# Turning the rounded tokens of a feed-forward stage by transposing transfers, with two banks for the down product and the loads ahead on ScalarE's queue

## The chip, the core and the metric

The kernel runs on one core of a Trainium2 chip. A core has TensorE (PE, matrix products, results in PSUM banks), VectorE (DVE), ScalarE (ACT), GpSimd (POOL) and SyncE (SP), which each run their own list of instructions in order and meet through semaphores. Transfers are issued from an engine's queue and carried out by 16 DMA engines that all queues share. The metric is the time of one execution in microseconds of the device, the median of several runs.

## The reference

Two transformer layers on x of 8 x 256 tokens x 512. Each layer is x + attention(layernorm(x)), then x + feed-forward(layernorm(x)); layer 0 has multi-head causal cross-attention and a quantised feed-forward network, layer 1 has latent attention and a mixture of 8 experts. The change lies in layer 0's feed-forward network:

```python
def _act_quant(x):
    scale = 127.0 / jnp.clip(jnp.max(jnp.abs(x), axis=-1, keepdims=True), 1e-05)
    return jnp.clip(jnp.round(x * scale), -128.0, 127.0) / scale      # its value
def _weight_quant(w):
    scale = 1.0 / jnp.clip(jnp.mean(jnp.abs(w)), 1e-05)
    return jnp.clip(jnp.round(w * scale), -1.0, 1.0) / scale          # its value
def _bitlinear(x, w):
    return jnp.einsum('bsd,fd->bsf', _act_quant(x), _weight_quant(w))
h = jax.nn.silu(_bitlinear(x, W1))      # 512 -> 2048
return _bitlinear(h, W2)                # 2048 -> 512
```

## The kernel before

The program is a row of blocks with a barrier between them. `layer0_attention` is followed by `layer0_feed_forward`, which first rounds both weight matrices (`quantise_weights`) and then works through the tokens. After it come `layer1_attention`, whose first block (`score_weights`, L1065) waits for four large weights loaded ahead (`ahead_in`), and `layer1_experts`.

The feed-forward block has 16 tiles of 128 tokens. Its order is written out by hand: each engine runs `step(t, par)` for t from -3 to 15 (L915), and `has(t, n)` says whether tile t + n exists. For a tile:

- GpSimd normalises it into `y` (L1001). VectorE takes the largest absolute value of each token, works out the scale and rounds the tile to `xq`, 128 x 512 in bf16 (`quantise_tokens`, L1025 to L1034), three steps ahead.
- TensorE turns the four 128 x 128 pieces of `xq` into the PSUM tile `xT` (L969), at the end of a step, and ScalarE copies them to `xqT` (L994). The copy is the stationary operand of the up product.
- TensorE makes the up product, 16 matmuls into four PSUM banks (L954), two steps ahead. Each half waits until ScalarE has taken the half before out of the bank (`silued`). ScalarE applies Silu with the scale (L990).
- VectorE reduces the hidden units to a maximum (L1021, 128 x 2048) and makes their scale; ScalarE scales them and adds a constant that rounds (`hr`, L984); VectorE takes the constant off (`hq`, L1039). TensorE turns `hq` in 16 pieces into `hT` (L944), ScalarE copies these in two halves to `hqT` (L979).
- TensorE makes the down product, 16 matmuls into the bank `down` (L963). VectorE scales it and adds it to the tokens (L1016), then takes the new statistics (L105, L107).

So TensorE's step is: turn hidden t, up t + 2, down t, turn tokens t + 3. VectorE's step is: add the output t - 1, maximum and scale of the hidden t + 1, round tokens t + 3, round hidden t + 1, statistics t - 1. SP issues only the four loads ahead (L932 to L935), at the block's head.

Of the kernel before, what the change touches and what calls it, by code (L numbers as in the profile page):

```python
# [13 lines left out]
BF16 = mybir.dt.bfloat16  # L14
U32 = mybir.dt.uint32
ALU = mybir.AluOpType
ACT = mybir.ActivationFunctionType
AX = mybir.AxisListType

P = 128  # L20
B, S, D = 8, 256, 512
TPB = S // P
TILES = B * TPB
DC = D // P
CTX = 128
DMA = 16
# [5 lines left out]
FC = F // P  # L32
# [849 lines left out]
def layer0_feed_forward(nc, io, X, mv, rstd, identb, store, w1_raw, w1_in, ahead, ahead_in):  # L882
    with Memory(nc, "b") as m:
        w2_raw = store.place("w2_raw", 8, [P, FC, D])
        w1, w2 = store.place("w1", 18, [P, DC, F], BF16), store.place("w2", 22, [P, FC, D], BF16)
# [6 lines left out]

        y, yr = [m.sb(f"y{i}", [P, D]) for i in range(2)], m.sb("yr", [P, D])
        xq = [m.sb(f"xq{i}", [P, D], BF16) for i in range(2)]
        xqT = m.sb("xqT", [P, DC, P], BF16)
        s1, s2 = m.sb("s1", [P, 2]), m.sb("s2", [P, 2])
        h = [m.sb(f"h{i}", [P, F]) for i in range(2)]
        hr, hq = m.sb("hr", [P, F]), m.sb("hq", [P, F], BF16)
        hqT = m.sb("hqT", [P, FC, P], BF16)
        amax, unit, q_scale = m.sb("amax", [P, 2]), m.sb("unit", [P, 2]), m.sb("q_scale", [P, 2])  # L900
        stats = m.sb("stats", [P, 6])
        up = m.ps("up", [P, F])
        xT = m.ps("xT", [P, DC, P], BF16)
        hT = m.ps("hT", [P, FC, P], BF16)
        down = m.ps("down", [P, D])
        y_ready, x_quant, x_turned, x_copied = m.sem("y_ready"), m.sem("x_quant"), m.sem("x_turned"), m.sem("x_copied")
        upped, silued = m.sem("upped"), m.sem("silued")
        h_scaled, h_rounded, h_quant = m.sem("h_scaled"), m.sem("h_rounded"), m.sem("h_quant")
        h_turned, h_copied, downed, added = m.sem("h_turned"), m.sem("h_copied"), m.sem("downed"), m.sem("added")
        HALF = FC // 2  # L910

        def all_steps(eng, step):


            for t in range(-3, TILES):  # L915
                step(t, t % 2)

        def has(t, ahead):

            return 0 <= t + ahead < TILES  # L920

        def after(eng, sem, n):

            if n > 0:
                eng.wait_ge(sem, n)

        with m.block() as block:
            @block.sync
            def _(sp):

                wq, kcq, wqr, kckv = ahead
                sp.dma_start(kcq, io["kcq"].rearrange("h (c p) k -> p h c k", p=P)).then_inc(ahead_in, DMA)  # L932
                sp.dma_start(wqr, io["wqr"].rearrange("h (c p) r -> p h c r", p=P)).then_inc(ahead_in, DMA)
                sp.dma_start(wq, io["wq1"].rearrange("(h k) d -> k h d", k=P)).then_inc(ahead_in, DMA)
                sp.dma_start(kckv, io["kckv"].rearrange("h k d -> k h d")).then_inc(ahead_in, DMA)  # L935

            @block.tensor
            def _(pe):
                def step(t, par):
                    if has(t, 0):  # L940
                        pe.wait_ge(h_quant, t + 1)
                        after(pe, h_copied, 2 * t)
                        for c in range(FC):
                            last = pe.transpose(hT[:, c, :], hq[:, c * P:(c + 1) * P], identb[:, :])  # L944
                            if c == HALF - 1:
                                last.then_inc(h_turned, 1)
                        last.then_inc(h_turned, 1)
                    if has(t, 2):
                        pe.wait_ge(x_copied, t + 3)
                        for n in range(4):  # L950
                            if n % 2 == 0:
                                after(pe, silued, 2 * t + 3 + n // 2)
                            for c in range(DC):
                                last = pe.matmul(up[:, n * D:(n + 1) * D], xqT[:, c, :], w1[:, c, n * D:(n + 1) * D],  # L954
                                                 start=c == 0, stop=c == DC - 1)
                            if n % 2:
                                last.then_inc(upped, 1)
                    if has(t, 0):
                        after(pe, added, t)
                        for c in range(FC):  # L960
                            if c % HALF == 0:
                                pe.wait_ge(h_copied, 2 * t + 1 + c // HALF)
                            last = pe.matmul(down[:, :], hqT[:, c, :], w2[:, c, :], start=c == 0, stop=c == FC - 1)  # L963
                        last.then_inc(downed, 1)
                    if has(t, 3):
                        pe.wait_ge(x_quant, t + 4)
                        after(pe, x_copied, t + 3)
                        for c in range(DC):
                            last = pe.transpose(xT[:, c, :], xq[1 - par][:, c * P:(c + 1) * P], identb[:, :])  # L969
                        last.then_inc(x_turned, 1)  # L970
                all_steps(pe, step)

            @block.scalar
            def _(act):
                def step(t, par):
                    if has(t, 0):
                        for i in range(2):
                            act.wait_ge(h_turned, 2 * t + i + 1)
                            act.activation(hqT[:, i * HALF:(i + 1) * HALF, :], hT[:, i * HALF:(i + 1) * HALF, :], ACT.Copy  # L979
                                           ).then_inc(h_copied, 1)  # L980
                    if has(t, 1):
                        act.wait_ge(h_scaled, t + 2)
                        after(act, h_quant, t + 1)
                        act.activation(hr[:, :], h[1 - par][:, :], ACT.Copy, scale=q_scale[:, 1:2], bias=MAGIC  # L984
                                       ).then_inc(h_rounded, 1)
                    if has(t, 2):
                        for n in range(2):
                            act.wait_ge(upped, 2 * t + n + 5)
                            cols = slice(n * F // 2, (n + 1) * F // 2)
                            act.activation(h[par][:, cols], up[:, cols], ACT.Silu, scale=s1[:, par:par + 1]  # L990
                                           ).then_inc(silued, 1)
                    if has(t, 3):
                        act.wait_ge(x_turned, t + 4)
                        act.activation(xqT[:], xT[:], ACT.Copy).then_inc(x_copied, 1)  # L994
                all_steps(act, step)

            @block.gpsimd
# [7 lines left out]
            def _(dve):  # L1005
                def scales(i):

                    dve.drain()
                    dve.tensor_scalar(unit[:, i:i + 1], amax[:, i:i + 1], 1e-5, 1.0 / 127.0, ALU.max, ALU.mult)
                    dve.drain()  # L1010
                    return dve.reciprocal(q_scale[:, i:i + 1], unit[:, i:i + 1])

                def add_output(t, par):
                    dve.wait_ge(downed, t + 1)
                    xt = X[:, t, :]
                    dve.scalar_tensor_tensor(xt, down[:, :], s2[:, par:par + 1], xt, ALU.mult, ALU.add  # L1016
                                             ).then_inc(added, 1)

                def scale_hidden(t, par):
# [3 lines left out]
                    dve.tensor_scalar(s2[:, par:par + 1], unit[:, 1:2], mean[:, 1:2], None, ALU.mult)  # L1023

                def quantise_tokens(t, par):  # L1025
                    after(dve, x_turned, t - 1)
                    dve.wait_ge(y_ready, t + 1)
                    dve.tensor_reduce(amax[:, 0:1], y[par][:, :], AX.X, ALU.max, apply_absolute_value=True)
                    scales(0)
                    dve.tensor_scalar(s1[:, par:par + 1], unit[:, 0:1], mean[:, 0:1], None, ALU.mult)  # L1030
                    dve.drain()
                    dve.tensor_scalar(yr[:, :], y[par][:, :], q_scale[:, 0:1], MAGIC, ALU.mult, ALU.add)
                    dve.drain()
                    dve.tensor_scalar(xq[par][:, :], yr[:, :], -MAGIC, 127.0, ALU.add, ALU.min).then_inc(x_quant, 1)  # L1034
# [9 lines left out]
                def step(t, par):  # L1044
                    if has(t, -1):
                        add_output(t - 1, 1 - par)
                    if has(t, 1):
                        scale_hidden(t + 1, 1 - par)
                    if has(t, 3):
                        quantise_tokens(t + 3, 1 - par)  # L1050
                    if has(t, 1):
                        quantise_hidden(t + 1)
                    else:
                        dve.drain()
                    if has(t, -1):
                        new_stats(t - 1)
                all_steps(dve, step)
                add_output(TILES - 1, (TILES - 1) % 2)
                dve.drain()
                new_stats(TILES - 1)  # L1060
# [836 lines left out]
```

## Time and profile before

| | us |
|---|---|
| median of 3 runs | 1128.49 (1125.04 to 1131.27) |
| the profiled execution | 1127.68 |
| its span, first to last instruction | 1125.9 |
| TensorE busy in the span | 994.8 (88%) |
| VectorE, ScalarE busy | 763.1 (68%), 651.4 (58%) |
| GpSimd busy | 283.4 (25%) |
| feed-forward block, from its first load's issue to its last output add | 325.64 to 471.51 |

A row of the timeline gives the start, the length, the engine, the line, the operation, what it writes and reads, and how many instructions are merged; in brackets stands how long the engine was idle before it and what released it. A matmul's end is modelled, so the start of the next group on TensorE is the better mark. A row of the stretches gives the busy time of each engine with its count, the granted clock of TensorE as a share of the full one, the share of the DMA engines, and GB/s.

### The profile page before, as it was taken

To read this page: it belongs to the slowest core of one execution; us is meant where nothing else is said; L and a number is where in the kernel's file an instruction comes from. 1 tells how busy PE (TensorE), PEld (TensorE's weight loads), DVE (VectorE), ACT (ScalarE), POOL (GpSimd) and SP (SyncE) were. 2 spreads that over 40 slices of the span, in tenths; PEclk is the share of its full clock that TensorE was granted. 3 is DMA by queue.
4 is the path that set the end of the run, shared out by engine and by line. 5 is a ranking of instruction groups with operands and counts; after the bars stand their busy time and mean duration, and the time that the engine had idled before them with its cause. 6 is when DMAs were issued, how large, how long until landed. Compare 5 with 4: busy or idle time off the path is not lost. (4 is left out here: it accounts for less than half of the span.)

```text
span 1125.9 us, 20668 instructions
## 1 busy us (share of the span) xinstructions
PE 994.8 (88%) x7516; PEld 782.9 (70%) x7516; DVE 763.1 (68%) x1654; ACT 651.4 (58%) x1691; POOL 283.4 (25%) x276
## 2 busy tenths in 40 slices
PE   5799999997129999886999999899998999999586
PEld 5678888876014555534888888788887888888485
DVE  6757666664757998435676767577775767777466
ACT  4657777765547878454555555355554555555275
POOL 5765565343033332021001010010101001000372
PEclk9989999999659999987999999999999999999889
DMA  7210000000438000141000000000000000000013
GB/s 263 98 67 6 7 2 2 2 1 1 149 105 249 1 1 2 38 169 57 1 1 19 2 20 2 3 20 1 20 1 23 1 1 1 1 1 2 0 39 113
DMA packets 20091, 41.95 MB, mean 37 GB/s; under 512 B 1168, under 2 KB 4496, under 8 KB 19472
## 3 DMA queue, kind: packets, MB, share of 16 engines
q1 hardware_dynamic: 19984, 40.53, 10.8%
q8 instruction: 67, 1.10, 0.4%
q14 instruction: 40, 0.33, 0.1%
HBM read 36.33 MB, written 4.19 MB: 36 GB/s over the span
## 5 line engine op out<-in xcount | busy, mean ns | idle before, releaser
L1214 POOL TENSOR_TENSOR c_ctx_raw<-c_ctx_raw,c_table 128x1024 f32<-128x1024 f32 x8 | 19.0, 2379 | 448.7 <-PE c_bank_b L1358 366.5
L1440 ACT ACTIVATE probs<-c_score,c_neg_max 128x256 f32<-128x256 f32 x256 | 119.2, 480 | 15.4 <-DVE c_neg_max L1501 15.4
L1426 ACT ACTIVATE c_h<-c_bank_b 128x512 fp32r<-128x512 f32 x64 | 38.3, 598 | 153.6 <-PE c_bank_b L1358 153.6
L559 POOL TENSOR_TENSOR a_probs<-a_probs,a_inv 128x256 f32<-128x256 f32 (+1 forms) x128 | 102.7, 830 | 90.5 <-DVE a_inv L660 90.4
L451 ACT ACTIVATE a_probs<-a_s,a_neg_max 128x128 f32<-128x128 f32 (+1 forms) x256 | 104.4, 435 | 32.3 <-DVE a_neg_max L648 31.9
L1491 DVE TENSOR_TENSOR c_l<-c_bank_b,c_h 128x512 fp32r<-128x512 f32 x64 | 44.3, 692 | 99.2 <-ACT c_h L1426 99.2
L1431 ACT ACTIVATE c_pT_h<-c_turn 128x512 fp32r<-128x512 f32 x128 | 69.9, 596 | 63.4 <-PE c_turn L1348 63.4
L44 PE MATMUL c_acc<-VO_h,c_l 128*128 128x512 f32 x256 | 100.9, 394 | 1.9 <-DVE c_l L1491 1.9
L46 PE MATMUL c_acc<-VO_h,c_h 128*128 128x512 f32 x256 | 100.5, 393 | 0.0
L45 PE MATMUL c_acc<-VO_l,c_h 128*128 128x512 f32 x256 | 100.0, 391 | 0.0
L1501 DVE TENSOR_REDUCE c_neg_max<-c_score 128x2 f32<-128x512 f32 x128 | 82.0, 682 | 9.7 <-PE c_score L1337 8.8
L1496 DVE TENSOR_TENSOR c_pT_l<-c_turn,c_pT_h 128x512 fp32r<-128x512 f32 x128 | 82.1, 681 | 2.3 <-ACT c_pT_h L1431 2.3
L44 PE MATMUL c_bank_a<-c_yT_h,A_l 128*128 128x256 f32 x256 | 78.3, 306 | 1.4 <-DVE c_yT_l L1482 1.4
L1509 DVE TENSOR_SCALAR probs<-probs,c_inv 128x256 f32<-128x256 f32 x256 | 75.7, 359 | 5.1
L45 PE MATMUL c_bank_a<-c_yT_l,A_h 128*128 128x256 f32 x256 | 73.1, 286 | 0.0
L46 PE MATMUL c_bank_a<-c_yT_h,A_h 128*128 128x256 f32 x256 | 72.9, 285 | 0.0
L1348 PE MATMUL c_turn<-g_ident,probs 128*128 128x128 f32 x512 | 72.1, 286 | 0.7 <-DVE probs L1509 0.7
L648 DVE TENSOR_REDUCE a_neg_max<-a_s 128x2 f32<-128x256 f32 (+1 forms) x128 | 63.5, 549 | 10.5 <-PE a_s L317 9.9
L1001 POOL TENSOR_SCALAR b_y<-g_x,g_mean_var,g_rstd 128x512 f32<-128x512 f32 x16 | 44.3, 2768 | 100.6 <-DVE b_xq L1034 65.4
L1487 DVE TENSOR_TENSOR c_qk_l<-c_bank_a,c_qk_h 128x512 fp32r<-128x512 f32 x64 | 44.0, 687 | 29.9 <-ACT c_qk_h L1422 29.7
L1348 PEld LDWEIGHTS c_turn<-g_ident,probs 128*128 128x128 f32 x512 | 57.2, 144 | 8.8 <-DVE probs L1509 1.4
L954 PE MATMUL b_up<-w,b_xqT 128*128 128x512 bf16 x256 | 60.9, 393 | 2.2 <-ACT b_xqT L994 2.2
(253 smaller groups left out, 2866.6 us busy)
## 6 DMA issues: line engine op xcount, KB each, us to landing
w_raw<-in_w SPq DMA_DIRECT2D x1, 4096.0 KB, 13.8
w_raw<-in_w SPq DMA_DIRECT2D x4, 1024.0 KB, 8.8
wq<-in_wq SPq DMA_DIRECT2D x1, 4096.0 KB, 22.8
c_ctx_raw<-in_ctx SPq DMA_DIRECT2D x8, 512.0 KB, 3.6
wo<-in_wo SPq DMA_DIRECT2D x1, 4096.0 KB, 14.3
out<-g_x SPq DMA_DIRECT2D x16, 256.0 KB, 2.1
g_x<-in_x SPq DMA_DIRECT2D x7, 512.0 KB, 6.6
wq_raw<-in_wq SPq DMA_DIRECT2D x4, 256.0 KB, 4.5
```

The source lines that it names most:

```text
L44: pe.matmul(out, ll, rh, start=start and n == 0, stop=False)
L45: pe.matmul(out, lh, rl, start=False, stop=False)
L46: last = pe.matmul(out, lh, rh, start=False, stop=stop and n == len(pairs) - 1)
L451: last = act.activation(probs[i % 2][:, 2 * pair + j, at], s[:, 2 * pair + j, at], ACT.Exp, bias=neg_max[:, pair, q, j:j + 1], accum_out=s ...
L559: last = pool.tensor_tensor(p, p, inv[:, pair, q, :].unsqueeze(2).broadcast_to([P, 2, (q + 1) * P]), ALU.mult)
L648: last = dve.tensor_reduce(neg_max[:, pair, q, :], s[:, 2 * pair:2 * pair + 2, q * P:(2 * q + 1) * P], AX.X, ALU.max, negate=True)
L1348: last = pe.transpose(turn[k][:, hq * P:(hq + 1) * P], probs[p % 2][:, hq, k * P:(k + 1) * P], ident[:, :])
L1431: act.activation(pT_h[:, k, :], turn[k][:, :], ACT.Copy).then_inc(turn_hi, 1)
L1440: last = act.activation(probs[p % 2][:, i, :], score[h][:, t, :], ACT.Exp, bias=neg_max[:, i:i + 1], accum_out=sums[:, i:i + 1])
L1496: dve.tensor_tensor(pT_l[:, k, :], turn[k][:, :], f32(pT_h[:, k, :]), ALU.subtract).then_inc(turn_lo, 1)
L1501: dve.tensor_reduce(neg_max[:, 2 * h:2 * h + 2], score[h][:, :, :], AX.X, ALU.max, negate=True).then_inc(maxed, 1)
L1509: last = dve.tensor_scalar(probs[p % 2][:, i, :], probs[p % 2][:, i, :], inv[:, i:i + 1], None, ALU.mult)
```

## The change

1. The four 128 x 128 pieces of a rounded token tile are turned by four transfers with `transpose=True` that SP issues, straight into `xqT`, which now has two buffers. TensorE's token transposes, the PSUM tile `xT`, ScalarE's copy and the semaphore `x_copied` go. `x_turned` becomes two semaphores, one for each buffer, that count 16 for each transfer. The up product waits for four transfers of its tile; SP waits for the rounding, and for the up product two tiles earlier before it writes its buffer again.
2. The down product alternates between two PSUM banks, and so waits for the output add of two tiles earlier.
3. The four loads ahead are issued from ScalarE's queue, ahead of its first step, and no longer from SP's.

The hidden units are turned by TensorE as before.

```diff
-        xqT = m.sb("xqT", [P, DC, P], BF16)
+        xqT = [m.sb(f"xqT{i}", [P, DC, P], BF16) for i in range(2)]
...
-        xT = m.ps("xT", [P, DC, P], BF16)
         hT = m.ps("hT", [P, FC, P], BF16)
-        down = m.ps("down", [P, D])
+        down = [m.ps(f"down{i}", [P, D]) for i in range(2)]
...
+        X_TURN = DC * DMA
...
             @block.sync
             def _(sp):
 
-                wq, kcq, wqr, kckv = ahead
-                sp.dma_start(kcq, io["kcq"].rearrange("h (c p) k -> p h c k", p=P)).then_inc(ahead_in, DMA)
...
+                for t in range(TILES):
+                    sp.wait_ge(x_quant, t + 1)
+                    after(sp, upped, 2 * (t - 1))
+                    for c in range(DC):
+                        sp.dma_start(xqT[t % 2][:, c, :], xq[t % 2][:, c * P:(c + 1) * P], transpose=True).then_inc(x_turned[t % 2], DMA)
...
                     if has(t, 2):
-                        pe.wait_ge(x_copied, t + 3)
+                        pe.wait_ge(x_turned[par], ((t + 2) // 2 + 1) * X_TURN)
...
-                        after(pe, added, t)
+                        after(pe, added, t - 1)
...
-                            last = pe.matmul(down[:, :], hqT[:, c, :], w2[:, c, :], start=c == 0, stop=c == FC - 1)
+                            last = pe.matmul(down[par][:, :], hqT[:, c, :], w2[:, c, :], start=c == 0, stop=c == FC - 1)
                         last.then_inc(downed, 1)
-                    if has(t, 3):
-                        pe.wait_ge(x_quant, t + 4)
-                        after(pe, x_copied, t + 3)
-                        for c in range(DC):
-                            last = pe.transpose(xT[:, c, :], xq[1 - par][:, c * P:(c + 1) * P], identb[:, :])
-                        last.then_inc(x_turned, 1)
...
-                    if has(t, 3):
-                        act.wait_ge(x_turned, t + 4)
-                        act.activation(xqT[:], xT[:], ACT.Copy).then_inc(x_copied, 1)
+
+                wq, kcq, wqr, kckv = ahead
+                act.dma_start(kcq, io["kcq"].rearrange("h (c p) k -> p h c k", p=P)).then_inc(ahead_in, DMA)
+                act.dma_start(wqr, io["wqr"].rearrange("h (c p) r -> p h c r", p=P)).then_inc(ahead_in, DMA)
+                act.dma_start(wq, io["wq1"].rearrange("(h k) d -> k h d", k=P)).then_inc(ahead_in, DMA)
+                act.dma_start(kckv, io["kckv"].rearrange("h k d -> k h d")).then_inc(ahead_in, DMA)
                 all_steps(act, step)
...
                 def quantise_tokens(t, par):
-                    after(dve, x_turned, t - 1)
+                    after(dve, x_turned[t % 2], t // 2 * X_TURN)
```

The order of ScalarE's instructions at the block's head, of the kernel before, with what each waits for:

```order
L973 UNCONDITIONAL_BRANCH [waits barrier_Pool_Activation_PE_DVE_SP_release]
L994 ACTIVATE b_xqT<-b_xT 128x512 [waits b_x_turned]
L990 ACT_TABLE_LOAD
L990 ACTIVATE b_h<-b_up,b_s 128x1024 [waits b_upped] x2
L994 ACTIVATE b_xqT<-b_xT 128x512 [waits b_x_turned]
L984 ACTIVATE b_hr<-b_h,b_q_scale 128x2048 [waits b_h_scaled]
```

and of the changed kernel, at the same place:

```order
L967 UNCONDITIONAL_BRANCH [waits barrier_Pool_Activation_PE_DVE_SP_release]
L988 DMA kcq<-in_kcq 128x48x128
L989 DMA wqr<-in_wqr 128x48x64
L990 DMA wq_50<-in_wq 128x16x512
L991 DMA kckv<-in_kckv 128x16x128
L984 ACT_TABLE_LOAD
L984 ACTIVATE b_h<-b_up,b_s 128x1024 [waits b_upped] x2
L978 ACTIVATE b_hr<-b_h,b_q_scale 128x2048 [waits b_h_scaled]
```

The four loads stand ahead of the loading of the Silu table and of the first Silu; the copies of the turned tokens are gone.

SP's list at the same place, the difference from before to after:

```order
 L928 UNCONDITIONAL_BRANCH [waits barrier_Pool_Activation_PE_DVE_SP_release]
-L932 DMA kcq<-in_kcq 128x48x128
-L933 DMA wqr<-in_wqr 128x48x64
-L934 DMA wq_50<-in_wq 128x16x512
-L935 DMA kckv<-in_kckv 128x16x128
+L935 DMA_TRANSPOSE b_xqT<-b_xq 128x128 [waits b_x_quant]
+L935 DMA_TRANSPOSE b_xqT<-b_xq 128x128 x3
+L935 DMA_TRANSPOSE b_xqT<-b_xq 128x128 [waits b_x_quant]
+L935 DMA_TRANSPOSE b_xqT<-b_xq 128x128 x3
+L935 DMA_TRANSPOSE b_xqT<-b_xq 128x128 [waits b_upped,b_x_quant]
+L935 DMA_TRANSPOSE b_xqT<-b_xq 128x128 x3
```

SP's queue now holds 64 transposing transfers, four for each of the 16 tiles, the first of each tile behind the waits.

TensorE's list from the head into the first full step, the difference from before to after:

```order
 L937 UNCONDITIONAL_BRANCH
-L969 MATMUL b_xT<-g_identb,b_xq 128x128 x4
-L954 MATMUL b_up<-w_4887,b_xqT 128x512 x16
-L969 MATMUL b_xT<-g_identb,b_xq 128x128 x4
-L954 MATMUL b_up<-w_4887,b_xqT 128x512 x16
-L969 MATMUL b_xT<-g_identb,b_xq 128x128 x4
+L954 MATMUL b_up<-w_4887,b_xqT 128x512 x32
 L944 MATMUL b_hT<-g_identb,b_hq 128x128 x16
 L954 MATMUL b_up<-w_4887,b_xqT 128x512 x16
 L963 MATMUL b_down<-w_4888,b_hqT 128x512 x16
-L969 MATMUL b_xT<-g_identb,b_xq 128x128 x4
 L944 MATMUL b_hT<-g_identb,b_hq 128x128 x16
```

Nothing else moves: a full step is the hidden turn, up and down, now without the four token transposes behind them.

## Rows read from the trace of the kernel before

**Rows 1.** The page: its span.
```profile
span 1125.9 us, 20668 instructions
```
**Rows 2.** Stretches: PE, PEld, DVE, ACT, POOL busy (count), clock, DMA share, GB/s.
```profile
362.00:459.00 97.00, 97.00 (x638) 51.67 (x637) 85.40 (x163) 77.28 (x73) 27.90 (x10) 1.00 0.00 1
459.00:466.00 7.00, 4.71 (x36) 2.42 (x34) 4.82 (x8) 3.97 (x4) 0.00 (x0) 1.00 0.00 0
```
**Rows 3.** Timeline of one period, TensorE, then VectorE.
```profile
387.23 3.62 PE L954 MATMUL b_up<-w,b_xqT 128*128 128x512 bf16 x16
...
394.13 0.39 PE L969 MATMUL b_xT<-g_identb,b_xq 128*128 128x128 bf16 x4
394.36 1.06 PE L944 MATMUL b_hT<-g_identb,b_hq 128*128 128x128 bf16 x16
395.25 3.62 PE L954 MATMUL b_up<-w,b_xqT 128*128 128x512 bf16 x16
...
394.34 0.75 DVE L1016 SCALAR_TENSOR_TENSOR g_x<-b_down,b_s,g_x 128x512 f32<-128x512 f32 x1 [0.27 <-PE b_down L963]
...
399.67 0.43 DVE L1034 TENSOR_SCALAR b_xq<-b_yr 128x512 bf16<-128x512 f32 x1
```
**Rows 4.** Waits between 360 and 460 us: total, times, longest.
```profile
ACT b_hr L984 <- DVE b_q_scale L1011: 9.5, 12, 0.8
ACT b_xqT L994 <- PE b_xT L969: 9.5, 12, 0.8
```
**Rows 5.** Timeline of SP's queue at the block's head.
```profile
325.64 0.84 SPq L932 DMA_DIRECT2D kcq<-in_kcq  x1
326.93 9.24 SPq L933 DMA_DIRECT2D wqr<-in_wqr  x1
...
344.84 4.21 SPq L935 DMA_DIRECT2D kckv<-in_kckv  x1
```
**Rows 6.** Timeline of ScalarE at the block's head.
```profile
331.25 0.60 ACT L994 ACTIVATE b_xqT<-b_xT 128x512 bf16<-128x512 bf16 x1 [5.92 <-PE b_xT L969]
331.87 1.28 ACT L990 ACT_TABLE_LOAD   x1
335.36 1.11 ACT L990 ACTIVATE b_h<-b_up,b_s 128x1024 f32<-128x1024 f32 x1 [2.21 <-PE b_up L954]
337.09 1.11 ACT L990 ACTIVATE b_h<-b_up,b_s 128x1024 f32<-128x1024 f32 x1 [0.61 <-PE b_up L954]
```
**Rows 7.** Timeline of VectorE and TensorE, from the head to the last period.
```profile
338.23 2.29 DVE L1021 TENSOR_REDUCE b_amax<-b_h 128x1 f32<-128x2048 f32 x1 [5.02 <-ACT b_h L990]
338.74 3.63 PE L954 MATMUL b_up<-w,b_xqT 128*128 128x512 bf16 x16 [1.47 <-ACT b_xqT L994]
...
342.91 0.43 DVE L1034 TENSOR_SCALAR b_xq<-b_yr 128x512 bf16<-128x512 f32 x1
...
345.58 5.14 PE L954 MATMUL b_up<-w,b_xqT 128*128 128x512 bf16 x16
...
350.56 3.62 PE L963 MATMUL b_down<-w,b_hqT 128*128 128x512 bf16 x16
...
454.87 3.62 PE L963 MATMUL b_down<-w,b_hqT 128*128 128x512 bf16 x16
```
**Rows 8.** Transfers: queue instructions by line, issues by source, to landing.
```profile
L1615 SPq DMA_DIRECT2D out<-g_x x16: 332/332/375, 1087.8 to 1123.4; - x16
...
DMA to landing us min/median/max: 2.0/2.1/2.9
...
L123 SPq DMA_DIRECT2D w_raw<-in_w x4: 379/500/1262, 287.0 to 288.5; - x4
...
g_ident<-in_ident SPq DMA_DIRECT2D x1, 64.0 KB, 3.0
...
kckv<-in_kckv SPq DMA_DIRECT2D x1, 0.5 KB, 17.6
g_iota<-in_iota SPq DMA_DIRECT2D x1, 4.0 KB, 3.2
```

More of the change, by code:

```diff
@@ L902, in layer0_feed_forward @@
         up = m.ps("up", [P, F])
-        xT = m.ps("xT", [P, DC, P], BF16)
         hT = m.ps("hT", [P, FC, P], BF16)
-        down = m.ps("down", [P, D])
-        y_ready, x_quant, x_turned, x_copied = m.sem("y_ready"), m.sem("x_quant"), m.sem("x_turned"), m.sem("x_copied")
+        down = [m.ps(f"down{i}", [P, D]) for i in range(2)]
+        y_ready, x_quant, x_turned = m.sem("y_ready"), m.sem("x_quant"), [m.sem(f"x_turned{i}") for i in range(2)]
         upped, silued = m.sem("upped"), m.sem("silued")
@@ L929, in _ @@
             def _(sp):
-                wq, kcq, wqr, kckv = ahead
-                sp.dma_start(kcq, io["kcq"].rearrange("h (c p) k -> p h c k", p=P)).then_inc(ahead_in, DMA)
-                sp.dma_start(wqr, io["wqr"].rearrange("h (c p) r -> p h c r", p=P)).then_inc(ahead_in, DMA)
-                sp.dma_start(wq, io["wq1"].rearrange("(h k) d -> k h d", k=P)).then_inc(ahead_in, DMA)
-                sp.dma_start(kckv, io["kckv"].rearrange("h k d -> k h d")).then_inc(ahead_in, DMA)
+                for t in range(TILES):
[3 more added lines that the diff above has]
+                        sp.dma_start(xqT[t % 2][:, c, :], xq[t % 2][:, c * P:(c + 1) * P], transpose=True).then_inc(x_turned[t % 2], DMA)
             @block.tensor
@@ L953, in step @@
                             for c in range(DC):
-                                last = pe.matmul(up[:, n * D:(n + 1) * D], xqT[:, c, :], w1[:, c, n * D:(n + 1) * D],
+                                last = pe.matmul(up[:, n * D:(n + 1) * D], xqT[par][:, c, :], w1[:, c, n * D:(n + 1) * D],
                                                  start=c == 0, stop=c == DC - 1)
@@ L1015, in add_output @@
                     xt = X[:, t, :]
-                    dve.scalar_tensor_tensor(xt, down[:, :], s2[:, par:par + 1], xt, ALU.mult, ALU.add
+                    dve.scalar_tensor_tensor(xt, down[par][:, :], s2[:, par:par + 1], xt, ALU.mult, ALU.add
                                              ).then_inc(added, 1)
```

## The prediction

> **What bounds the kernel now.** I read the page first, then the busy time by stretches, one period of the feed-forward block in the timeline, its waits, and last the queues at the block's head. The profiled execution took 1127.68 us, of which 1125.9 are the span [rows 1]; the median of the three runs is 1128.49, so a sum made on the profile stands 0.8 us under it. The change touches one of four blocks, from the start of its loads at 325.64 [rows 5] on. From 362 to 459 TensorE is busy 97.00 of 97.00 us at the full granted clock, VectorE 85.40, ScalarE 77.28 [rows 2]. A tile takes 395.25 - 387.23 = 8.02 us there, from up product to up product; between lie down, the turning of the tokens (4 matmuls, 394.13) and that of the hidden units (394.36) [rows 3]. So the 4 token transposes own 0.23 us of a period. VectorE is close behind: it waits 0.27 us for down in this period, which leaves it 7.75 of its own. ScalarE waits for TensorE and for VectorE, 0.8 us each per tile [rows 4]. At the head it is different: ScalarE's first two Silus end at 338.20 and VectorE, idle until then, starts its maximum at 338.23 [rows 6, 7]. The head is a chain of dependences and not a full engine.
>
> **Turning off TensorE and ScalarE.** 16 x 4 transposes and 16 copies (0.60 us each) go. Only the TensorE part lies on the path: from the down at 350.56 to that at 454.87 there are 13 periods (104.31 / 13 = 8.02) [rows 7], times 0.23 = 3.0 us, if nothing takes its place. The copies stood in a ScalarE that waits 0.8 us twice in a period [rows 4]: nothing. The second bank for down is worth nothing, since VectorE's add (0.75 us from 394.34) is done long before the next down, which follows the up of 395.25.
>
> **The wait that comes instead.** up now waits for four transfers that SP issues once VectorE has rounded the tile. (SP's own second wait, for the up two tiles back, is over by then: that up ended in the period before.) Call L the time from the end of the rounding to the landing of the fourth. The rounding of rows 3 ends at 399.67 + 0.43 = 400.10; the up that used it started one period after 395.25, at 403.27. L must be under 3.17 us to keep 8.02, and under 2.7 for a period of 7.79. If it is longer, a ring closes: up starts at 387.23, down after it, VectorE's add at 394.34, then maximum and scale of the hidden units, then the rounding that ends at 400.10 and serves the up two tiles on. That is 12.87 us plus L for two tiles. A period is (12.87 + L) / 2, and each us of L over 3.17 costs half a us per tile. Behind this wait on TensorE stand up, down and the next hidden turn; VectorE's add waits for that down.
> No transposing transfer is in the trace. The nearest rows are plain transfers of SP's queue: issue 0.33 us at the shortest (output), 1.26 at the longest and 0.50 in the middle (w_raw); landing 2.0 at the shortest (output), 3.0 for 64 KB and 3.2 for 4 KB inward [rows 8]. Four in a row have three issues ahead of the last: L from 3 x 0.33 + 2.0 = 3.0 to 3 x 1.26 + 3.2 = 7.0. I take 3 x 0.50 + 3.0 = 4.5, the middle issue and the inward transfer nearest in size to a piece of 32 KB. Then (12.87 + 4.5) / 2 = 8.69, which is 0.67 over 8.02, times 13 = **+8.7 us** (ends: -1.1 at L = 3.0; +24.9 at 7.0, a period of 9.94). VectorE's 7.75 shortens nothing: it waits for down, which waits for up. The clock should hold: at 459 to 466, with TensorE busy 4.71 of 7.00 us, it was still granted 1.00, the upper of its two levels, 2.4 GHz [rows 2].
> The Trainium skill ("DMA: Bandwidth & Descriptors", Anatomy of one DMA) gives every transfer a fixed part of about 2.0 us, mostly the receipt of the last byte; this trace agrees with its 2.0 to 3.2 us [rows 8]. By 2.0 alone an estimate of L would be 3.5 and of the period 8.19.
>
> **The loads move in front of ScalarE's work.** SP issued the four loads from 325.64 to 344.84 + 4.21 = 349.05, and the second issue alone held the queue 9.24 us [rows 5]. SP had nothing else to do, so that was free. Now the same four stand in ScalarE's stream ahead of its table load and its first Silu. ScalarE works in order, so its table load starts at 349.05, not 331.87, and the Silus end at 349.05 + 1.28 + 2 x 1.11 = 352.55, not 338.20 [rows 6]. VectorE's maximum moves from 338.23 to about 352.55: **+14.3 us**. TensorE meanwhile has tile 0's up done and idles, so tile 1's up may run at the lower clock level, 5.14 us as the up at 345.58 [rows 7] did; started behind the first Silu at 351.4 it ends at 356.6, and the old end, 338.74 + 3.63, moved by 14.3 is 356.7: nothing is added. Nor does tile 0's turning show: it has until about 345. Bounds of this term: 14.3 if the queue holds ScalarE as it held SP; 0 if each issue is as short as the first (0.84), since four of those lie within the 5.92 us that ScalarE sat idle here [rows 6]. I take 14.3, since bytes, descriptors and the 16 DMA engines are the same.
> The Trainium skill says against this ("DMA: Bandwidth & Descriptors", Issuing engines are not separate DMA queues) that issuing from several engines saves only the sequencer's time, "which is usually small relative to the DMA itself". The row says otherwise: 23.4 us of issuing, with the last byte at 362.4. By the page the move would cost ScalarE little; that is case (b).
>
> **Turning while the loads run.** The DMA engines are in use until kckv lands at 344.84 + 17.6 = 362.4 [rows 5, 8]. Tile 2's rounding, ended at 343.34, and its up, at 345.58 [rows 7], both move by 14.3, to 357.6 and 359.9: 2.2 us for an L among loads. Its lower end is 3.0 (+0.8); its upper end, as long as that load's own landing, 17.6, is +15. I take 4.8, a little over the free case, since the pieces are small: **+2.6 us**. Later tiles are turned after 362.
>
> Sum: 1127.68 + 14.3 + 2.6 + 8.7 = 1153.3 as an execution like the profiled one, and 0.8 more against the median: **1154 us**.
>
> **Rivals.**
> (a) Transposing transfers are slow or follow each other one by one. At 2 us apart and 3.0 to land, L = 9.0, the period is 10.94, and +37.9 takes the place of 8.7: 1182. For it: a queue instruction can last 9.24 us when the engines are full, and nothing in the trace shows a transpose. Against: 32 KB each on idle engines (share 0.00 from 362 to 459 [rows 2]). It begins at L = 6, 1163 us.
> (b) ScalarE isn't held by its queue: 1127.68 + 2.6 + 8.7 = 1139.0. For it: only the first issue, 0.84 us, met free engines, and ScalarE's queue is otherwise empty. Against: the second issue waited with nothing ahead of it but the first.
> (c) The change does all that it removes and nothing comes instead, the case that isn't slower: ScalarE not held and L at most 2.7. TensorE's period falls to 7.79, just above VectorE's 7.75: 1127.68 - 3.0 = 1124.7. It needs four transfers issued and landed in 2.7 us where single ones took 2.0 to 3.2.
>
> **How the numbers follow.** Forecast (held, L of 3.0 to 6.0, own range 1141 to 1163): 0.57. (a): 0.25. (b): 0.13. (c): 0.05. The range from 1137 to 1176 takes in most of (b) and the nearer half of (a), and leaves out about 2 in 10. A measurement of this kernel tells 0.5%, 5.6 us, from no change: faster is under 1122.8, slower over 1134.1. (c) and the shortest of (b) are within: 0.07. Under 1122.8 lies no case: 0.02. Slower: 0.91.
>
> **What will show it.** Four issue rows on ScalarE's queue that end near 349 and the first Silu at about 350.3. TensorE idle ahead of up, released by a transfer of xqT, some 0.9 us a tile; the down products 8.7 us apart; ScalarE's wait for TensorE's token turn gone; TensorE's share of the stretch under 1. A turned piece landing in about 3 us. I am wrong if the first Silu starts before 340, if the issue rows on ScalarE are short, if the period is under 8.0 or over 9.5, or if the granted clock in the block's middle falls below 1.00.

## The result, and the profile after

The changed kernel takes 1173.48 us (median of 4 runs, 1170.78 to 1179.13) beside 1126.76 us of the kernel before (4 runs): a ratio of 1.0422, with a 95% interval of 1.036 to 1.0484. It is slower. The time lies in the forecast range, but the step is +46.7 us where 25.5 were forecast.

The page of the profiled execution after (1171.65 us) begins so; PEclk in its second part is the granted clock in 40 slices, in tenths. The second fence is the same row of the kernel before.

```profile
span 1169.9 us, 20586 instructions
...
PEclk9999999997568889898799999999999999999798
```

```profile
PEclk9989999999659999987999999999999999999889
```

Slices 14 to 16 lie in the block's middle in both: 9 9 9 before, 8 8 9 after. Over 105 us there the granted clock is 0.91 after (columns as in [rows 2], where it is 1.00):

```profile
385.00:490.00 105.00, 88.07 (x483) 42.59 (x482) 72.53 (x142) 60.59 (x50) 25.98 (x9) 0.91 0.06 13
```

The span grew by 44.0 us from that of [rows 1]. I cut both spans at the first GpSimd normalisation of the block (325.64 before, 321.19 after) and at the end of its last output add (471.51, 516.80). What lies ahead of the block is the same program in both and differs by 4.5 us in the other direction (over the eleven kernels of this document the block starts between 321.2 and 325.6); what lies behind is 654.4 and 653.1 us. The block itself went from 145.9 to 195.6: **+49.7 us**, the whole loss. Its head, up to the first down product, went from 24.9 to 45.7 (+20.8); the 13 periods from the first down to the fourteenth from 104.3 to 133.3 (+29.0); its tail is 16.6 in both. The two down products that bound the periods after (before: [rows 7]):

```profile
366.86 3.62 PE L963 MATMUL b_down<-w,b_hqT 128*128 128x512 bf16 x16
...
500.15 3.62 PE L963 MATMUL b_down<-w,b_hqT 128*128 128x512 bf16 x16
```

The head, in ScalarE's timeline of the kernel after; it answers to [rows 5, 6]:

```profile
321.19 0.87 ACTq L988 DMA_DIRECT2D kcq<-in_kcq  x1
...
322.52 9.62 ACTq L989 DMA_DIRECT2D wqr<-in_wqr  x1
332.17 10.48 ACTq L990 DMA_DIRECT2D wq<-in_wq  x1
...
342.86 4.37 ACTq L991 DMA_DIRECT2D kckv<-in_kckv  x1
347.26 1.28 ACT L984 ACT_TABLE_LOAD   x1 [4.43 <-issue]
348.56 2.12 ACT L984 ACTIVATE b_h<-b_up,b_s 128x1024 f32<-128x1024 f32 x2
```

ScalarE does nothing for 26.0 us but hand over loads. Its first two Silus end 29.5 us into the block, where they ended 12.6 us into it before.

Two tiles of the steady part, TensorE and VectorE's rounding in the timeline after; they answer to [rows 3]:

```profile
434.73 3.62 PE L954 MATMUL b_up<-w,b_xqT 128*128 128x512 bf16 x16
...
438.18 3.62 PE L963 MATMUL b_down<-w,b_hqT 128*128 128x512 bf16 x16
...
439.37 0.43 DVE L1031 TENSOR_SCALAR b_xq<-b_yr 128x512 bf16<-128x512 f32 x1
...
441.64 1.06 PE L944 MATMUL b_hT<-g_identb,b_hq 128*128 128x128 bf16 x16
...
445.89 5.31 PE L954 MATMUL b_up<-w,b_xqT 128*128 128x512 bf16 x16 [3.19 <-DMA b_xqT<-b_xq]
...
451.04 3.62 PE L963 MATMUL b_down<-w,b_hqT 128*128 128x512 bf16 x16
...
455.39 3.62 PE L954 MATMUL b_up<-w,b_xqT 128*128 128x512 bf16 x16
```

The rounding ends at 439.80 and the up that needs it starts at 445.89: L is 6.09 us, read up to the start of that up. The wait comes at every other tile. A tile with it takes 12.86 us from down to down (438.18 to 451.04), one without it 7.80 (451.04 to 458.84), the period that had been worked out for a TensorE without its token transposes. And the up behind the wait lasts 5.31 us, not 3.62. The stretches show the granted clock (columns as in [rows 2]):

```profile
441.80:445.80 4.00, 0.89 (x16) 0.72 (x13) 3.81 (x6) 2.46 (x3) 1.08 (x1) 1.00 0.11 25
445.80:447.50 1.70, 1.61 (x7) 0.66 (x7) 1.40 (x6) 1.49 (x1) 0.00 (x0) 0.82 0.00 0
447.50:451.00 3.50, 3.50 (x11) 1.35 (x10) 2.02 (x4) 1.11 (x1) 2.98 (x1) 0.60 0.09 19
451.00:454.00 3.00, 3.00 (x15) 1.37 (x14) 0.00 (x0) 1.11 (x1) 0.00 (x0) 1.00 0.13 27
```

After TensorE's idle 3.2 us the granted clock falls, in the up that follows, to a mean of 0.60 over 3.5 us, most of it at the lower of its two levels (1.2 GHz), and is back at 1.00 (2.4 GHz) with the down behind it. The 16 matmuls pay 1.7 us.

The transposing transfers themselves, from the view of the tile xqT of the kernel after; [rows 8] held only plain ones:

```profile
L935 SPq DMA_TRANSPOSE b_xqT<-b_xq x64: 1093/1232/1936, 326.1 to 492.6; - x64
...
DMA to landing us min/median/max: 2.2/2.3/9.5
```

So 3 x 1.23 + 2.3 = 6.0 us, the L of the timeline.

### The profile page after: what moved, and what is told of

Its sections match the earlier page's. It is cut to its first block and busy times, and to the rows that moved or that the text cites. A ratio compares the mean times of both kernels' runs of the same rounds, so it can differ in the third digit from the quotient of the medians.

```text
span 1169.9 us, 20586 instructions
## 1 busy us (share of the span) xinstructions
PE 1001.1 (86%) x7452; PEld 777.5 (66%) x7452; DVE 766.3 (66%) x1654; ACT 645.4 (55%) x1678; POOL 283.1 (24%) x276
## 5 line engine op out<-in xcount | busy, mean ns | idle before, releaser
L954 PE MATMUL b_up<-w,b_xqT 128*128 128x512 bf16 x256 | 74.5, 457 | 59.9 <-DMA b_xqT<-b_xq 52.7
L954 PEld LDWEIGHTS b_up<-w,b_xqT 128*128 128x128 bf16 x256 | 28.1, 114 | 100.6 <-DMA b_xqT<-b_xq 54.0
L1506 DVE TENSOR_SCALAR probs<-probs,c_inv 128x256 f32<-128x256 f32 x256 | 79.1, 373 | 5.1
```

What stands on the lines that cost most here:

```text
L954: last = pe.matmul(up[:, n * D:(n + 1) * D], xqT[par][:, c, :], w1[:, c, n * D:(n + 1) * D], start=c == 0, stop=c == DC - 1)
L1506: last = dve.tensor_scalar(probs[p % 2][:, i, :], probs[p % 2][:, i, :], inv[:, i:i + 1], None, ALU.mult)
```

## The experiments

Two theories stand against each other. The first has four causes that add: ScalarE held at the head, the latency L in a ring through VectorE, the clock that falls in the waits, and a turning that is slow beside the loads. The main rival is that the loads, moved and mixed with the turning, make all of it. In the table, head, 13 periods and block are in us as defined above, from the profiled execution; the ratio is to the kernel before, measured beside each.

| kernel | median us | ratio (95%) | head | 13 periods | block |
|---|---|---|---|---|---|
| before (four medians) | 1126.76 to 1128.34 | 1 | 24.9 | 104.3 | 145.9 |
| after | 1173.48 | 1.0422 (1.036 to 1.0484) | 45.7 | 133.3 | 195.6 |
| e1_loads_on_scalar | 1144.85 | 1.0157 (1.011 to 1.0204) | 41.8 | 104.3 | 164.4 |
| e2_loads_spread | 1166.74 | 1.0348 (1.0309 to 1.0388) | 38.8 | 133.8 | 189.2 |
| e3_one_transfer | 1149.01 | 1.02 (1.0155 to 1.0244) | 33.7 | 115.6 | 167.6 |
| e4_fill_the_wait | 1167.47 | 1.0368 (1.0307 to 1.0429) | 39.9 | 131.3 | 187.8 |
| e5_one_bank | 1171.06 | 1.0422 (1.0389 to 1.0455) | 38.9 | 133.7 | 189.2 |
| e6_loads_last | 1202.47 | 1.0668 (1.065 to 1.0685) | 33.7 | 133.1 | 183.5 |
| e7_one_transfer_loads_last | 1156.95 | 1.0266 (1.0247 to 1.0285) | 26.8 | 101.4 | 144.8 |
| e8_round_earlier | 1136.16 | 1.0086 (1.0062 to 1.0111) | 35.1 | 102.9 | 154.6 |
| e9_one_earlier_late_loads | 1124.67 | 0.9984 (0.9963 to 1.0006) | 26.5 | 102.4 | 147.2 |

**e1_loads_on_scalar.** The kernel before, with the loads' queue changed alone.

```diff
-                sp.dma_start(kcq, ...)      # and wqr, wq, kckv
+                act.dma_start(kcq, ...)     # and wqr, wq, kckv, ahead of all_steps(act, step)
```

> The kernel before with one part of the change: the four loads ahead are issued from ScalarE's queue instead of SP's; tokens are still turned by TensorE. Theory (the queue holds ScalarE as it held SP, 23.4 us from first to last issue): the first Silus end about 14 us later in the block, everything after is shifted, 1127 + 14 = 1141 us. Rival (in the changed kernel ScalarE was held because transposing transfers ran beside the loads): the issues are short here, first Silus at most 3 us later, 1127 to 1130 us.

+16.5 us (1144.85 to 1128.34). ScalarE's timeline in it:

```profile
324.16 0.88 ACTq L993 DMA_DIRECT2D kcq<-in_kcq  x1
...
325.49 9.43 ACTq L994 DMA_DIRECT2D wqr<-in_wqr  x1
334.95 8.17 ACTq L995 DMA_DIRECT2D wq<-in_wq  x1
...
343.34 4.03 ACTq L996 DMA_DIRECT2D kckv<-in_kckv  x1
347.42 0.60 ACT L990 ACTIVATE b_xqT<-b_xT 128x512 bf16<-128x512 bf16 x1 [4.11 <-issue]
```

The queue holds ScalarE for 23.2 us, as it held SP for 23.4 [rows 5], with no transposing transfer anywhere; the rival is out. It costs more than the 14 expected, since here the copy of the first turned tile stands behind the loads too, and the first up starts only behind it, at 348.47. The periods are untouched, 104.3.

**e2_loads_spread.** The changed kernel, with each load issued by ScalarE in a step of its own.

```diff
+                far = {-3: (kcq, ...), 1: (wqr, ...), 3: (wq, ...), 6: (kckv, ...)}
                 def step(t, par):
+                    if t in far:
+                        act.dma_start(*far[t]).then_inc(ahead_in, DMA)
```

> The changed kernel with its four loads issued by ScalarE one at a time, in steps -3, 1, 3 and 6, so that each meets an idle queue. Theory (two causes that add: ScalarE held at the head, and a ring closed by L = 6.1 us with a slow up product behind each long wait): issues under 1 us each, the head as in the kernel before within 4 us, 20.7 us for two tiles as in the changed kernel, so 13 x (10.3 - 8.0) = +30 and about 1157 to 1160 us. Rival (the loads are the cause of the whole loss, later tiles suffer from a late start): within 5 us of the kernel before.

The issues are short now:

```profile
322.91 0.89 ACTq L977 DMA_DIRECT2D kcq<-in_kcq  x1
361.97 0.73 ACTq L977 DMA_DIRECT2D wqr<-in_wqr  x1
382.37 0.42 ACTq L977 DMA_DIRECT2D wq<-in_wq  x1
415.86 0.72 ACTq L977 DMA_DIRECT2D kckv<-in_kckv  x1
```

The periods stay at 133.8, so the hold explains nothing of them. But the head fell only by 6.9, to 38.8, and the time is 7 us over the upper end that I had expected. The first tile was rounded at 327.82 and its up began at 339.46, 11.6 us later: four transfers beside kcq's load, which landed at 338.6. My head, "as before within 4 us", was a miss.

**e3_one_transfer.** As e2, with one transfer for a tile.

```diff
-                    for c in range(DC):
-                        sp.dma_start(xqT[t % 2][:, c, :], xq[t % 2][:, c * P:(c + 1) * P], transpose=True)...
+                    sp.dma_start(xqT[t % 2][:, :, :], xq[t % 2][:, :], transpose=True)...
```

> As e2_loads_spread, but one transposing transfer of 128 x 512 turns a tile in place of four of 128 x 128. Theory A (the 1.23 us in the queue are paid once for each instruction): L = about 1.2 + 2.3 = 3.5 us, the ring gives (12.9 + 3.5) / 2 = 8.2 us a tile, no long wait of TensorE and so no slow up, 1128 to 1133 us. Theory B (the queue's time goes by the blocks turned, 0.15 us for each 16 x 128 block): one issue holds 4.9 us, L stays near 6, 1157 us as e2_loads_spread.

```profile
L934 SPq DMA_TRANSPOSE b_xqT<-b_xq x16: 1189/1191/1308, 329.8 to 468.2; - x16
...
DMA to landing us min/median/max: 2.3/2.3/10.1
```

One instruction that turns 128 KB holds the queue 1.19 us and lands 2.3 us after its issue, the same as one that turns 32 KB. Theory A holds for the price, B is out, and L is 2.3 to 2.4 with no load beside it, shorter still than the 3.5 that I had added up: the 2.3 us to the landing include the 1.2 in the queue. Outside the loads the tiles follow at 7.80 us. The time is 16 us over what A expected. The block is 21.7 us longer than before's: 8.8 in the head, where tile 0 landed 10.2 us after its rounding, beside kcq's load; 11.3 in the periods; 1.7 in a last down at the lower clock. The waits in TensorE's timeline say where those of the periods are:

```profile
385.42 3.60 PE L953 MATMUL b_up<-w,b_xqT 128*128 128x512 bf16 x8 [6.48 <-DMA b_xqT<-b_xq]
...
414.64 5.31 PE L953 MATMUL b_up<-w,b_xqT 128*128 128x512 bf16 x15 [2.88 <-DMA b_xqT<-b_xq]
```

They stand right behind the issues of wq (374.64) and kckv (407.51). A transposing transfer beside a load lands late, up to 10.1 us, and the ring has no slack for that.

**e4_fill_the_wait.** As e2, with one bank for down, and matmuls in TensorE's wait; their result is not used.

```diff
+                        for _ in range(14 if t >= 0 and t % 2 == 0 else 0):
+                            pe.matmul(fill[:, :], w1[:, 0, 0:P], w1[:, 0, 0:D], start=True, stop=True)
                         pe.wait_ge(x_turned[par], ((t + 2) // 2 + 1) * X_TURN)
```

> As e2_loads_spread, with one bank for the down product and, in the bank that this frees, 14 matmuls of 128 x 512 on TensorE ahead of the wait for the turned tokens of tiles 2, 4, ... 14 (their result is not used), about 3.0 us, within the 3.2 us that TensorE waits there. Theory (the up product behind the wait runs slow because TensorE's clock falls in the wait): up takes 3.6 us in place of 5.0 to 6.4, 19.0 us for two tiles in place of 20.7, 10 us less than e2_loads_spread. Rival (up is slow for another reason, such as its operand just landed): same time as e2_loads_spread, up still over 5 us.

```profile
439.95 3.19 PE L950 MATMUL b_fill<-w 128*128 128x512 bf16 x13
443.31 3.63 PE L956 MATMUL b_up<-w,b_xqT 128*128 128x512 bf16 x16 [0.18 <-DMA b_xqT<-b_xq]
...
458.92 3.19 PE L950 MATMUL b_fill<-w 128*128 128x512 bf16 x13
462.81 3.63 PE L956 MATMUL b_up<-w,b_xqT 128*128 128x512 bf16 x16 [0.70 <-DMA b_xqT<-b_xq]
```

The up behind a filled wait takes 3.63 us with its operand just landed, so the slow up is the clock's doing and not its operand's. The granted clock around such an up, the one at 424.34, is 1.00:

```profile
423.90:428.00 4.10, 3.76 (x18) 1.68 (x18) 3.60 (x9) 2.79 (x2) 2.01 (x1) 1.00 0.04 8
```

The ring closes as worked out: from the up at 424.34 to the rounding that ends at 437.22 are 12.88 us, plus an L of 6.09, and two tiles take 18.97 (to 443.31); the next pairs take 19.50 and 19.61, with L at 6.61 and 6.73, against 20.65 without the filling. In the whole time it does not show, 1167.47 beside 1166.74: the 13 periods are only 2.5 us shorter, and my expectation of 10 us less was a miss. The fillings don't fit everywhere; a wait of 6.58 us beside wq's load fell on an odd tile, which had none, and at the head they delay an up. So the mechanism is shown; its price over the block, 10 us, is read from the rows of the kernel after and not from a time.

**e5_one_bank.** As e2, with a single bank.

```diff
-        down = [m.ps(f"down{i}", [P, D]) for i in range(2)]
+        down = m.ps("down", [P, D])
-                        after(pe, added, t - 1)
+                        after(pe, added, t)
```

> As e2_loads_spread, with a single bank for the down product, which waits for the output add of the tile before. Theory (the second bank is worth nothing, the add is done 3 us or more ahead of the next down product): the same time as e2_loads_spread, 1163 to 1170 us, no wait of TensorE or of its weight loads ahead of down. Rival (the ring makes the add late, so the second bank hides part of it): 1 us or more a tile longer, over 1175.

1171.06 us, ratio 1.0422 (1.0389 to 1.0455) beside e2's 1.0348 (1.0309 to 1.0388). The medians lie 4 us apart, and e5's is 1 us over my upper end. In the profiled executions the blocks are equal, 189.2 us each, and the periods 133.7 and 133.8. In both, weight loads ahead of down wait 1.8 us in all for the add, twice. I read it as no effect of the bank in the block, from one execution of each. The rows can't say where the 4 us lie: e5's profiled execution, 1164.34 us, is the shortest of its six and shorter than e2's, 1165.91. What makes them stays open.

**e6_loads_last.** The changed kernel, with the four loads issued by ScalarE behind its last step. The next block waits for them, so only the block is to be compared.

```diff
-                act.dma_start(kcq, ...)     # and wqr, wq, kckv
                 all_steps(act, step)
+                act.dma_start(kcq, ...)     # and wqr, wq, kckv
```

> The changed kernel with its four loads issued by ScalarE behind its last step of the block, so that nothing runs beside the turning; the next block then waits for them (known price about 20 to 30 us there). Read the block alone. Theory (ring with L = 6.1 us and the clock fall): every even tile's up behind a 3.2 us wait, 20.7 us for two tiles from the head to the end, first down about 27 to 30 us after the block's start in place of 45.7 (before: 24.9). Rival (the waits come from the loads beside it): no wait over 1 us, 7.8 us a tile.

```profile
437.52 5.31 PE L954 MATMUL b_up<-w,b_xqT 128*128 128x512 bf16 x16 [3.20 <-DMA b_xqT<-b_xq]
...
458.18 5.31 PE L954 MATMUL b_up<-w,b_xqT 128*128 128x512 bf16 x16 [3.20 <-DMA b_xqT<-b_xq]
```

458.18 - 437.52 = 20.66 with nothing beside the turning, and 133.1 us for the 13 periods: they owe nothing to the loads. The head is 33.7 us, more than the 27 to 30 I expected: it alone, with neither hold nor loads, is 8.8 over before's, from 6.2 us between rounding and up at tile 0 (before: 1.4) and 6.1 at tile 2 (before: 2.2). The ups behind both are slow, but so were before's, 5.15 and 5.14 us, so the clock adds nothing there. The late loads cost 36 us behind the block in the profiled execution, not 20 to 30.

**e7_one_transfer_loads_last.** e6 with one transfer for a tile.

> As e6_loads_last, with one transposing transfer a tile. Theory (one instruction costs 1.2 us of queue and lands 2.3 us after its issue, whether it turns 32 KB or 128 KB, and is slow only beside the loads): L = 2.4 us, no wait of TensorE, 7.80 us a tile throughout, the block 3 to 4 us shorter than before's 145.9, then the late loads' price of 20 to 30 us behind it. Rival (the one transfer was also slowed by itself in e3_one_transfer): the waits of 2.9 and 6.5 us seen there come again.

```profile
351.76 3.62 PE L962 MATMUL b_down<-w,b_hqT 128*128 128x512 bf16 x16
...
453.16 3.62 PE L962 MATMUL b_down<-w,b_hqT 128*128 128x512 bf16 x16
```

No wait for a transfer over 0.3 us after the first tile; the 13 periods are 101.4 us, which is 13 x 7.80, and the block 144.8, 1.1 shorter than before's, where I had expected 3 to 4. The transposes' 0.23 us a tile are there, 2.9 us in the periods; the head, 1.9 longer than before's, takes most of them back. The time, 1156.95 us, is longer than before's by what follows: behind the block the profiled execution takes 691.7 us (before: 654.4), as the next block waits for the late loads. The waits of e3 did not come again, so they were the loads'.

**e8_round_earlier.** As e2, four transfers a tile, with VectorE four steps ahead and three buffers.

```diff
-            for t in range(-3, TILES):
+            for t in range(-4, TILES):
-                        quantise_tokens(t + 3, 1 - par)
+                        quantise_tokens(t + 4, par)
-        xqT = [m.sb(f"xqT{i}", [P, DC, P], BF16) for i in range(2)]
+        xqT = [m.sb(f"xqT{i}", [P, DC, P], BF16) for i in range(3)]
```

> As e2_loads_spread (four transfers a tile, loads one at a time in steps -3, 1, 3 and 6), but VectorE rounds the tokens four steps ahead and not three, with three buffers of turned tokens. Theory (the loss is latency in a ring, not the capacity of the queue: 4 x 1.23 = 4.9 us of 7.8): the wait goes, 7.8 us a tile outside the loads, and only what the loads add (an L of 9 to 12) may show; 1126 to 1140 us. Rival (the queue or the DMA engines can't keep up): still over 9 us a tile, 1160.

```profile
356.33 3.62 PE L963 MATMUL b_down<-w,b_hqT 128*128 128x512 bf16 x16
...
459.22 3.62 PE L963 MATMUL b_down<-w,b_hqT 128*128 128x512 bf16 x16
```

The queue carries what it did in e2, 64 transfers of 1.23 us each, and the periods fall from 133.8 to 102.9 us. One wait is left behind the head, 1.29 us beside a load. The loss in the periods was latency in a ring and not the capacity of a queue. The head is still 35.1, 10.1 over before's: tile 0 is turned beside kcq's load, and its up starts 15.9 us into the block where before's started 6.3 us into it.

**e9_one_earlier_late_loads.** e8 with one transfer for a tile and the loads in steps 0, 3, 6 and 10.

> As e8_round_earlier with one transposing transfer a tile and the loads moved to steps 0, 3, 6 and 10, so that the first tiles are turned with nothing beside them. Theory: no wait of TensorE for a transfer at all, 7.80 us a tile, the block 3 us shorter than before's, 1124 to 1126 us, level with the kernel before or just ahead. Rival (an L beside a load is longer than the 10.5 us that the deeper pipeline covers): waits at the steps of the loads, 1130 or more.

```profile
378.84 3.63 PE L953 MATMUL b_up<-w,b_xqT 128*128 128x512 bf16 x16 [0.62 <-DMA b_xqT<-b_xq]
```

The best form of the idea: 1124.67 us, 0.9984 of the kernel before (0.9963 to 1.0006), no difference that can be told. A single wait of 0.62 us is left, where I had expected none. Its block is 1.3 us longer than before's: the periods give 1.9, the head costs 1.6, and its last down ran at the lower clock (5.29 us), for 1.7.

## Why the prediction was right, and where it was not

The direction and the range held, the range with 2.5 us to spare. The likeliest case held in kind, a ScalarE held by its queue and a ring that closes, but the step was 1.8 times the forecast. 1173.48 us lies outside that case's own range, 1141 to 1163, and the L of 6.09 just inside case (a), which was to begin at 6. Two of the signs of being wrong that the prediction named came: the period, 133.3 / 13 = 10.25 us, is over 9.5, and the granted clock in the block's middle is under 1.00. That the number fell within the range is so in part luck: the range had been stretched for slower transfers, and a part of what filled it, 10.7 us, is a slower clock that no case had. And the block alone grew by 49.7; in the profiled executions 5.8 us of that are offset outside the block. By its steps, against the block's +49.7 us:

- **The term for the loads in front of ScalarE (+14.3)** was right in mechanism, and 2.6 short. The Silus end 16.9 us later in the block; the issues took 26.0 us with the turning beside them, where they took 23.2 in e1 without it. Case (b) is out: e1 shows these 23.2 us of issuing in ScalarE's own stream. The Trainium skill's "usually small relative to the DMA itself" ("DMA: Bandwidth & Descriptors", Issuing engines are not separate DMA queues) does not hold for these four loads one behind the other, 23.2 of the 35.8 us from the first issue to the last landing in e1; it does for each alone on an idle queue, 0.4 to 0.9 us in e2.
- **Turning while the loads run (+2.6)** was mis-sized too: the head holds 20.75 - 16.93 = 3.8 more, an L of 6.09 at tile 2 (355.82 to 361.91) where 4.8 was taken. It was short for another reason than the loads: 6.09 is the L of free engines too (e6, tile 2: 347.69 to 353.78). That tile 0's turning does not show was right here (11.0 us, ended long before the Silu), and only because ScalarE was held; with the hold gone, e2 shows it in full.
- **The ring (+8.7)** had the right form and a wrong L. The 12.87 us measured 12.88 in e4. L was 6.09, not 4.5: the issues cost 1.23 us each, near the upper end of the bound, where I took the middle of plain loads, and the landing was 2.3 rather than 3.0. With 6.09, two tiles take 18.96, and the block has six forced pairs and one free tile: 6 x 18.96 + 7.80 - 104.3 = +17.3. I had also counted 13 tiles at the mean instead of six pairs and a free one, which is worth 0.9 at the L of 4.5.
- **"The clock should hold"** was wrong, and is the largest thing left out. I read it from a stretch of 7 us in the tail that was granted 1.00, though my own [rows 7] held an up of 5.14 us, at 345.58, and I reckoned with the lower level at the head alone. The waits of 3.2 to 3.9 us each drew a slow up, 32.47 us for the six of the 13 periods where 21.72 are normal: +10.7. 17.3 + 10.7 = 28.0 of the 29.0 us measured; the rest goes with two of the six waits, whose L was 6.3 and 6.8. That the slow up comes from the clock, e4 shows; that the six add 10.7 us to the time is summed from rows.
- **The transposes' 0.23 us a tile and the 7.79 period** were right: 7.80 wherever nothing waits, 101.4 us for 13 periods in e7. Case (c) asked for an L under 2.7 and for a ScalarE not held. Both came in e7 (one transfer, loads last), but the head then takes 1.9 of the 2.9 us back, and the late loads cost more behind the block. In e9, with the loads spread, head and tail take more than the periods give.
- **The second bank at nothing** stands by the blocks of e5 and e2 in one execution each, and by them alone; the medians differ by 4 us, unexplained.

The Trainium skill's fixed part of about 2.0 us a transfer ("DMA: Bandwidth & Descriptors", Anatomy of one DMA) is given in that section for transfers that GpSimd issues. SP's transposing transfers, which it does not speak of, landed in 2.3 us in the middle, close to it. The prediction's estimate of L by it, 3.5 us, missed because it took 0.50 us for an issue, where each transposing instruction held SP 1.23 us; with that the same estimate would be 3 x 1.23 + 2.0 = 5.7.

## What to carry to other kernels

A transfer that replaces work on a full engine is paid in latency: find the ring that it closes, add its issues one behind the other to its landing, and compare with the slack. If it doesn't fit, start a step earlier, with one buffer more, and turn a whole tile in one instruction. Loads go on a queue whose engine has nothing else to do, or one at a time; a second large load right behind a first held the engine that issued it for 8.7 to 9.6 us here, and 0.7 us on an idle queue. And a stall of some us on TensorE is to be priced with the slow matmuls behind it.

## What the runs showed of the hardware

- A transposing transfer from SP's queue holds it about 1.2 us whether it turns 128 x 128 or 128 x 512 in bf16 (1.23 and 1.19 us in the middle), and lands 2.3 us after its issue, those 1.2 included, on free DMA engines.
- Beside large loads the same transfer landed at most 8.1 to 11.2 us after its issue, by kernel (9.5 after, 11.2 in e9); with none beside it, at most 4.1 in e6 and 2.5 in e7.
- The issue of wqr right behind kcq's held its queue 8.7 to 9.6 us, on SP's queue and on ScalarE's; alone on an idle queue it took 0.73 us (e2).
- After waits of 3.2 to 3.9 us TensorE's next 16 matmuls took 5.0 to 6.4 us in place of 3.6 (5.3 in the middle). With the wait filled by matmuls they took 3.6 (e4). After waits of 0.6 and 1.3 us in e9 and e8 they took 3.6 as well; of two waits of 2.1 us in e2, one was followed by 3.6 and one by 5.3.
